# Two chained 3x3 convolutions and an attention block: every convolution as fp32 matmuls on four 64x64 tiles

## The reference

```python
for _ in range(3):
    t = relu(conv3x3(x, w1) + b1)
    x = x + (1/3) * (conv3x3(t, w2) + b2)
x = relu(x)
q, k, v = split(qkv_w @ x)              # 8 heads of 8 channels
k, v = layernorm(k), layernorm(v)       # over the 8 channels of a head
kv = sum over pixels of k (x) v / (64*64)
ret = q @ kv + x
u = gelu(o1_w @ ret)
out = gelu(o2_w @ u + x)
```

## Time and profile before

| quantity | value |
|---|---|
| median of the runs | 1623.48 us |
| span of the profiled execution | 1619.8 us |
| PE busy | 1581.7 us (98%) |
| VectorE (DVE) busy | 1090.7 us (67%) |
| ScalarE (ACT) busy | 751.2 us (46%) |
| GpSimd busy | 85.9 us (5%) |

### The profile page before, as it was taken

One profiled execution on the slowest core, in us unless ns is written; L12 is line 12 of the kernel. 1 busy time (PEld: TensorE's weight loads), 2 busy tenths in 40 slices (PEclk: granted clock), 3 DMA queues, 4 the chain that ended last, 5 costly groups with the idle time before them and its releaser, 6 DMA issues.

```text
span 1619.8 us, 25740 instructions
## 1 busy us (share of the span) xinstructions
PE 1581.7 (98%) x9339; PEld 1372.0 (85%) x9339; DVE 1090.7 (67%) x2060; ACT 751.2 (46%) x1322; POOL 85.9 (5%) x107
## 2 busy tenths in 40 slices
PE   7999999999999999999999999999999999999975
PEld 6999988888988889888898888988898879988862
DVE  5565687556875577765767667775587665876574
ACT  4333544436443464435643446433464334543454
POOL 0000000000000000000000000000000000000000
PEclk9999999999999999999999999999999999999997
DMA  6212332333322234122421235122531233112312
GB/s 114 53 26 53 53 53 40 62 57 53 66 40 53 53 55 77 27 52 53 80 52 27 52 66 92 27 39 49 90 60 27 40 59 59 27 27 53 69 37 52
DMA packets 149190, 85.98 MB, mean 53 GB/s; under 512 B 136652, under 2 KB 136652, under 8 KB 149068
## 3 DMA queue, kind: packets, MB, share of 16 engines
q0 software_dynamic: 13824, 50.34, 17.3%
...
## 4 chain that ended last, share of the span: by engine, by line
PE 93%; DVE 3%; ACT 2%; issue 1%; DMA 1%; SPq 0%; ACTq 0%; DVEq 0%
PE bank L930 30%; PE bank L889 18%; PE bank L891 16%; PE bank L890 16%; PE bank L977 4%; PE bank L989 4%; PE bank L1023 2%; PE bank L1036 2%; DMA out<-y_out 0%; SPq L387 0%; PE bank L1007 0%; DVE rstd L791 0%; ACT g L541 0%; DVE x_lo L652 0%; ACT x_in L536 0%
## 5 line engine op out<-in xcount | busy, mean ns | idle before, releaser
L889 PE MATMUL bank<-x_hi,w_hi 128*128 128x448 f32 (+2 forms) x1440 | 526.3, 365 | 3.5 <-DVE x_lo L652 3.3
L930 PE MATMUL bank<-v_all,fw 128*128 128x256 f32 x2304 | 517.1, 382 | 1.0 <-DVE v_all L731 0.6
L891 PE MATMUL bank<-x_hi,w_lo 128*128 128x448 f32 (+2 forms) x1440 | 509.3, 354 | 0.0
L890 PE MATMUL bank<-x_lo,w_hi 128*128 128x448 f32 (+2 forms) x1440 | 508.6, 353 | 0.0
L930 PEld LDWEIGHTS bank<-v_all,fw 128*128 128x128 f32 x2304 | 431.7, 190 | 73.7 <-ACT m L506 9.7
L889 PEld LDWEIGHTS bank<-x_hi,w_hi 128*128 128x128 f32 x1440 | 272.0, 189 | 48.3 <-issue 22.8
L891 PEld LDWEIGHTS bank<-x_hi,w_lo 128*128 128x128 f32 x1440 | 271.5, 189 | 15.2
L890 PEld LDWEIGHTS bank<-x_lo,w_hi 128*128 128x128 f32 x1440 | 271.6, 189 | 13.6
L493 ACT ACTIVATE t_eo<-bank,b_col 128x384 f32<-128x384 f32 (+2 forms) x240 | 141.6, 590 | 301.5 <-PE bank L891 300.9
L716 DVE TENSOR_TENSOR steps_q<-t_eo 128x1344 f32<-128x1344 f32 x96 | 119.9, 1249 | 193.4 <-ACT t_eo L493 193.4
L506 ACT ACTIVATE m<-bank 128x512 f32<-128x512 f32 x192 | 114.2, 602 | 167.7 <-PE bank L930 167.6
...
## 6 DMA issues: line engine op xcount, KB each, us to landing
...
out<-y_out SPq DMA_DIRECT2D x120, 128.0 KB, 2.7
...
b_col<-in_L_conv_b SPq DMA_DIRECT2D x4, 0.2 KB, 2.8
...
```

Source lines behind the costliest of these rows:

```text
L889: mm(ps, lhs[0], rhs[0], start=first, stop=False)
L890: mm(ps, lhs[0], rhs[1], start=False, stop=False)
L891: return mm(ps, lhs[1], rhs[0], start=False, stop=last)
L930: last = mm(ps, fw[:, q, 1 - stack, :], v_all[:, KEPT.index(q), g0 + stack:g0 + stack + size, :], start=stack == 0, stop=stack == 1)
```

## The change

**Layout.** The two images of a pair stand side by side in the partitions: image 0 in partitions 0 to 63, image 1 in 64 to 127, each with all its rows in the free dimension (`xs`, rows of 66 elements). The array is used as four independent 64x64 tiles.

**conv0** (`convolve_conv0`, line 703 of the new kernel). Nine taps, each a 64x64 fp32 matmul on 8 rows of 64 columns; the four tiles hold two images by two "sides", rows 8b.. from the top and rows from the bottom upwards. A block is 9 x 4 matmuls of 512 columns, in two parts of five and four taps; an image pair has four blocks. There are no high and low parts any more.

**conv1** (`convolve_conv1`, line 727). The transform now runs down the rows: four rows from six planes, three column taps each. A unit is two planes, that is 2 x 3 x 4 matmuls of 256 columns; three units are one half of the pair of images, and two halves are the whole. The upper side's data stand in partitions 0 to 63 and the lower side's in 64 to 127. VectorE transforms a half in seven instructions (lines 521 to 541) and combines a half in nine (lines 550 to 583), for both images together.

**Order.** No loop is left; everything is written out. `phases` names, for each round `it`, six phases over three pairs in flight: conv0 of the new pair's step 0, conv1 of the old pair's step 1, conv1 of the new pair's step 0, conv0 of the old pair's step 2, conv0 of the new pair's step 1, conv1 of the old pair's step 2. They have 8, 6, 6, 8, 8 and 6 gaps, 42 in all (0 to 41). Attention of pair it-2 follows the gaps by `LATE` (round 8, in which no new pair starts, by `LAST`; round 9 has attention alone). `TRANSFORMS` says at which gap VectorE transforms which half. The convolutions have two PSUM buffers of two banks, and PROJECT, UP and DOWN share one buffer of two banks (`ring_free`).

```diff
-CONV0_SIZES = (7, 7, 7, 6, 6)
...
+X_RING, V_RING = 3, 3
+PLANES = (1, 2, 3, 4, 0, 5)
...
+def phases(it):
+    new, old = it, it - 1
+    both = [(CONV0, new, 0), (CONV1, old, 1), (CONV1, new, 0), (CONV0, old, 2), (CONV0, new, 1), (CONV1, old, 2)]
+    return [p if 0 <= p[1] < PAIRS else None for p in both]
...
+TRANSFORMS = {5: (0, 0), 10: (0, 1), 25: (3, 0), 27: (3, 1), 33: (4, 0), 38: (4, 1)}
...
+LATE = {
+    1: steps(PIXELS, 0), 2: steps(PROJECT, 0) + steps(PIXELS, 1), 3: steps(PROJECT, 1), 4: steps(PROJECT, 2) + steps(PIXELS, 2),
+    5: steps(PROJECT, 3), 6: steps(PIXELS, 3), 7: steps(DEVIATION, 0), 8: steps(INVERT, 0), 9: steps(NORMALISE, 0, 1),
+    10: steps(NORMALISE, 2, 3) + steps(OUTER, 0), 11: steps(OUTER, 1, 2), 12: steps(OUTER, 3) + steps(PROJECT, 4),
+    14: steps(PROJECT, 5), 15: steps(RELU, 0), 16: steps(PROJECT, 6), 17: steps(RELU, 1), 18: steps(PROJECT, 7),
+    19: steps(DEVIATION, 1),
+    20: steps(INVERT, 1), 21: steps(NORMALISE, 4, 5), 22: steps(NORMALISE, 6, 7) + steps(OUTER, 4),
+    23: steps(OUTER, 5, 6), 24: steps(OUTER, 7), 25: steps(FOLD, 0), 26: steps(FOLD, 1), 27: steps(FOLD, 2),
+    28: steps(FOLD, 3) + steps(UP, 0), 29: steps(DOWN, 0) + steps(FINISH, 0),
+    30: steps(UP, 1), 31: steps(DOWN, 1) + steps(FINISH, 1), 32: steps(UP, 2), 33: steps(DOWN, 2) + steps(FINISH, 2),
+    34: steps(UP, 3), 35: steps(DOWN, 3) + steps(FINISH, 3),
+}
...
+            def drain_conv1(unit):
...
+                if part < 2:
+                    if part == 0 and half:
+                        act.wait_ge(sums_made, half)
...
+            def transform_t(unit, h, combined):
...
+                dve.wait_ge(drained, NUMBER[unit] + 1)
...
+                vec.tensor_tensor(q[:, :, :], rows[:, at + 2:at + 18, :], rows[:, at:at + 16, :], ALU.subtract
+                                  ).then_inc(t_read, 1)
...
+                vec.scalar_tensor_tensor(eo[:, :, :, :], centre, -4.0, ahead, ALU.mult, ALU.add).then_inc(t_read, 1)
...
+                vec.scalar_tensor_tensor(to[:, :, 2], step[:, :, 1], 2.0, step[:, :, 2], ALU.mult, ALU.add)
+                vec.scalar_tensor_tensor(to[:, :, 3], step[:, :, 1], -2.0, step[:, :, 2], ALU.mult, ALU.add)
+                vec.scalar_tensor_tensor(to[:, :, 4:6], step[:, :, 0:2], -4.0, step[:, :, 2:4], ALU.mult, ALU.add)
...
+                vec.tensor_tensor(to[:, :, 0], eo[:, :, 1, :], eo[:, :, 0, :], ALU.add)
+                vec.tensor_tensor(to[:, :, 1], eo[:, :, 1, :], eo[:, :, 0, :], ALU.subtract).then_inc(v_made, 1)
...
+            def combine_m(unit, h, transformed):
...
+                dve.wait_ge(drained, NUMBER[unit])
+                vec.tensor_tensor(sums[:, 0:2, :], m[:, 0:4:2, :], m[:, 1:4:2, :], ALU.add)
+                vec.tensor_tensor(sums[:, 2:4, :], m[:, 0:4:2, :], m[:, 1:4:2, :], ALU.subtract
+                                  ).then_inc(sums_made, 1)
...
+            for it, gap, unit, sub in GAPS:
+                if gap in TRANSFORMS and phases(it)[TRANSFORMS[gap][0]]:
+                    nth, h = TRANSFORMS[gap]
+                    transform_t((*phases(it)[nth], BLOCKS - HALVES + h), h, combined)
+                    transformed += 1
+                if unit and sub == 1:
+                    if unit[0] == CONV1 and unit[3] % PARTS == PARTS - 1:
+                        combine_m(unit, unit[3] // PARTS, transformed)
+                        combined += 1
...
+                for s in todo(it, gap):
+                    attention(it - 2, s)
...
-            def three(ps, lhs, rhs, first, last):
-                mm(ps, lhs[0], rhs[0], start=first, stop=False)
-                mm(ps, lhs[0], rhs[1], start=False, stop=False)
-                return mm(ps, lhs[1], rhs[0], start=False, stop=last)
+            def bank_free(unit):
+                if NUMBER[unit] >= 2:
+                    pe.wait_ge(drained, NUMBER[unit] - 1)
+            def convolve_conv0(unit, sub):
...
+                for tap in (range(0, 5), range(5, K * K))[sub]:
+                    r, c = tap // K, tap % K
+                    top = slice(8 * b + r, 8 * b + r + 8)
+                    last_row = ROWS - 1 - 8 * b + r
+                    bottom = slice(last_row, last_row - 8, -1)
+                    for side, rows in enumerate((top, bottom)):
+                        for p in range(2):
+                            half = slice(CH * p, CH * p + CH)
+                            last = mm(to[CH * side:CH * side + CH, BANK * p:BANK * p + BANK], w1_t[half, tap, :],
+                                      tile[half, rows, c:c + COLS], start=tap == 0, stop=tap == K * K - 1)
+                if sub == 1:
+                    last.then_inc(conv_ready, 1)
+            def convolve_conv1(unit):
+                _conv, a, s, k = unit
+                h, part = k // PARTS, k % PARTS
+                half = HALVES * FIRST[a, s] + h
+                if part == 0:
+                    if half == 0:
+                        pe.wait_ge(weights_made, 1)
+                    pe.wait_ge(v_made, half + 1)
+                bank_free(unit)
+                to = conv_ps[NUMBER[unit] % 2]
+                for j in range(2):
+                    place = 2 * part + j
+                    product = PLANES[place]
+                    for c in range(K):
+                        for i in range(2):
+                            for side in range(2):
+                                rows = slice(CH * side, CH * side + CH)
+                                tiles = slice(0, TILES) if side == 0 else slice(TILES - 1, None, -1)
+                                at = BANK * side + SPAN * j
+                                last = mm(to[CH * i:CH * i + CH, at:at + SPAN], fw[rows, product, c, :],
+                                          v[half % V_RING][rows, tiles, place, i, c:c + COLS],
+                                          start=c == 0, stop=c == K - 1)
+            def ring_free(a, s):
...
+                b, kind, k = RING[r - 1]
+                if kind == PROJECT:
+                    pe.wait_ge(proj_taken, 8 * b + k + 1)
+                elif kind == UP:
+                    pe.wait_ge(gelu_done, 4 * b + k + 1)
+                else:
+                    pe.wait_ge(down_added, 4 * b + k + 1)
```

More of the change, by code:

```diff
@@ L70 @@
[L70 to L106, removed]
@@ L109 @@
[L109 to L124, removed]
@@ L126 @@
[L126 to L146, removed]
@@ new lines @@
+UNITS = [unit for _it, _gap, unit, sub in GAPS if unit and sub == 1]
+NUMBER = {unit: n for n, unit in enumerate(UNITS)}
+CONV0S = [u[:3] for u in UNITS if u[0] == CONV0 and u[3] == 0]
+CONV1S = [u[:3] for u in UNITS if u[0] == CONV1 and u[3] == 0]
+assert [u[1:] for u in CONV0S] == [u[1:] for u in CONV1S]
+FIRST = {u[1:]: n for n, u in enumerate(CONV0S)}
+TRANSFORMS = {5: (0, 0), 10: (0, 1), 25: (3, 0), 27: (3, 1), 33: (4, 0), 38: (4, 1)}
+PIXELS, PROJECT, DEVIATION, INVERT, NORMALISE, OUTER, FOLD, UP, DOWN, FINISH, RELU = (
+    "pixels", "project", "deviation", "invert", "normalise", "outer", "fold", "up", "down", "finish", "relu")
@@ new lines, in steps @@
+def steps(kind, *numbers):
+    return [(kind, k) for k in numbers]
+LATE = {
[10 more added lines that the diff above has]
+}
@@ L185, in conv_attention_kernel, with todo @@
+def todo(it, gap):
+    table = LAST if it == PAIRS else LATE
+    return table.get(gap, []) if 0 <= it - 2 < PAIRS else []
+RING = [(it - 2, *s) for it, gap, _unit, _sub in GAPS for s in todo(it, gap) if s[0] in (PROJECT, UP, DOWN)]
+PROJECTED = (0, 1, 6, 7, 2, 3, 4, 5)
 def conv_attention_kernel(nc, x, w1, b1, w2, b2, qkv_w, o1_w, o2_w, kln_w, kln_b, vln_w, vln_b, out):
-    x_v = x.rearrange("(i k) c (j p) w -> i k p c j w", k=2, p=2)
-    out_v = out.rearrange("(i k) c (j p) w -> i k p c j w", k=2, p=2)
@@ L852, in _ @@
-            iteration(0, attends=False, splits=True, first=True)
-            with dve.Fori(1, PAIRS - 1) as i:
-                iteration(i, attends=True, splits=True)
-            iteration(PAIRS - 1, attends=True, splits=False)
-            attention(PAIRS - 1, LAST, RING_LAST)
+                for side, (near, far) in enumerate(((0, 2), (2, 0))):
+                    half = slice(CH * side, CH * side + CH)
+                    vec.tensor_copy(to[5][half], rows[far][half])
+                    last = vec.tensor_copy(g_first[half], rows[near][half])
@@ new lines, in _ @@
+            transpose_w1()
+            pe.wait_ge(w1_copied, 1)
+            for it, gap, unit, sub in GAPS:
+                if unit and unit[0] == CONV0:
+                    convolve_conv0(unit, sub)
+                elif unit:
+                    convolve_conv1(unit)
+                if (it, gap) == (0, 1):
+                    transpose_w2()
+                if (it, gap) == (0, 3):
+                    transpose_rest()
+                for s in todo(it, gap):
+                    attention(it - 2, s)
```

1147 lines of the change are left out of this document (455 added, 692 removed).

## The result

The changed kernel takes **1717.39 us** (median of four runs, 1716.16 to 1720.5) against 1623.64 us (1620.92 to 1625.59) of the kernel before in the same comparison. The ratio is 1.0582, with a 95% interval of 1.0565 to 1.0599: 5.8% slower, 3.4 us above the forecast of 1714. The profiled execution has a span of 1714.7 us, at a mean granted clock of 0.915.

A forecast was written before the change was run, and what follows sets the result against it. TensorE alone bounds the kernel. Rounds sum 99 + 154 + 1230 (six of 205: 165 work, 32 waits, 8 clock) + 130 + 97 = 1710 us span, with 3.7 around it 1714 us; eight-in-ten range 1590 to 1830.

The forecast's parts named there:

- (a): Gaps 10 and 11: TensorE waits before OUTER 0 and OUTER 2 for VectorE's NORMALISE chain, 12.3 us a round.
- (b): Gap 26: FOLD 1 waits for VectorE's copy after FOLD 0, behind the transform of gap 25, 4.1 us.
- (c): Gap 28: FOLD 3 waits behind the transform of gap 27, then UP 0 for the `gw` copy, 5.3 us.
- (d): Gap 34: UP 3 waits for VectorE's addition for DOWN 2, behind the transform of gap 33, 4.7 us.
- (e): Gap 41: ScalarE may not overwrite `m` until sums behind the transform of gap 38 are made, 5.8 us.
- clock: TensorE runs at half clock after each of five waits in a full round, costing 8 us.
- Round 1: Round without attention: 139.7 us of convolution plus waits at gaps 13 and 41 and clock, 154 us.
- Round 0: First round, no old pair: start near 7, 1.7 for cold clock, convolutions, exposed combination and transfer, ending at 99 us.
- Round 8: Round with no new pair: 62 us of convolution, 25.6 of attention, waits and some cold clock, 130 us.
- Rival 2: Convolutions: rows of 66 elements or four streams slow matmuls by 11%, 123 us on top, about 1800 us; chance 0.2.
- Rival 3: Convolutions: weight loads, 0.13 us in each four-tile round, come into the open, 450 us, total 2100; chance 0.06 (or worse).
- Rival 1: Middle rounds: no waits to speak of, 165 to 175 us each, 1478 us total; chance 0.22 with partial cases.

The follow-up runs named there:

- x7_both28: x3_last with VectorE's transform of gap 27 moved to gap 28, behind that gap's attention steps: 1514.31 us, ratio 0.9322 to the kernel before.
- x1_norm: Changed kernel with NORMALISE 2 and 3 moved from gap 10 to gap 9, ahead of the transform and combination: 1667.87 us.
- x5_gap10: Changed kernel with four unneeded VectorE reductions added ahead of the transform of gap 10 in rounds 2 to 7: 1739.09 us.
- x2_fold: Changed kernel with the transforms of gaps 25, 27 and 33 placed behind their gap's attention steps: 1633.97 us.
- x8_fold28: x2_fold with the transform of gap 27 moved to gap 28, behind that gap's attention steps: 1589.51 us.
- x3_last: Changed kernel with the transform behind combination and attention in every gap, and NORMALISE 0 to 3 at gap 9: 1549.0 us.
- x9_warm42: Changed kernel with 42 idle matmuls ahead of the wait before OUTER 2 in rounds 2 to 7: 1709.11 us.

## Why the prediction was right

**Bound and work.** The forecast rested on TensorE's work falling to 165 us a full round; PE is busy 168.74 in x7_both28's round, at full clock. The convolutions are exact where they stand alone (0.43 and 0.22 us a round of four). So is the attention: in x7_both28's round its steps, from start to start and without waits, sum to 25.8 us, where 25.6 stood. The 3.5 us missing lie in the convolution's groups next to a step of another tile shape. Eight rounds of conv0 take 3.43 us from start to start between UP and DOWN, and 3.61 between two PROJECTs:

```profile
541.79 3.63 PE L703 MATMUL ps<-xs,w_t 64*64 64x512 f32 x32
545.22 1.05 PE L802 MATMUL ps<-g,o 64*64 64x512 f32 x8
...
603.57 3.68 PE L703 MATMUL ps<-xs,w_t 64*64 64x512 f32 x32
607.18 1.16 PE L757 MATMUL ps<-kvw,y 64*128 64x128 f32 x16
```

The prediction had seen this cost (0.16 us at a change of shape) and then left it out of its sum for PROJECT, OUTER and FOLD.

**The waits**, term by term, per middle round:

| step | priced | measured | tested by |
|---|---|---|---|
| (a) OUTER 0 and 2 at gaps 10, 11 | 12.3 | 1.2 + 10.6 | x1_norm, x5_gap10 (the 10.6) |
| (b) FOLD 1 | 4.1 | 3.8 | x2_fold |
| (c) FOLD 3 and UP 0 | 5.3 | 4.6 + 0.3 | x2_fold, x8_fold28 |
| (d) UP 3 | 4.7 | 4.4 | x2_fold |
| (e) gap 41, `sums_made` | 5.8 | 2.15 | gone in x3_last and x7_both28, never moved alone |
| clock | 8 | 9.0 (PE busy 177.75, less 168.74 in x7_both28) | x9_warm42, for one place |

The waits sum to 27, not 32. **The mis-sized term is (e).** I let the whole transform of gap 38 wait for `conv_ready`. VectorE's timeline of the changed kernel says otherwise, and ScalarE's drain comes earlier for it:

```profile
639.59 2.35 DVE L521 TENSOR_TENSOR q<-t 128x2112 f32<-128x2112 f32 x1
641.85 1.25 DVE L528 SCALAR_TENSOR_TENSOR eo<-t 128x1056 f32<-128x1056 f32 x1
646.27 0.71 DVE L536 SCALAR_TENSOR_TENSOR v<-q 128x528 f32<-128x528 f32 x1 [3.17 <-PE ps L727]
...
651.06 1.22 DVE L551 TENSOR_TENSOR sums<-m 128x1024 f32<-128x1024 f32 x1
```

```profile
652.37 0.69 ACT L392 ACTIVATE m<-ps,b_third 128x512 f32<-128x512 f32 x1 [5.07 <-DVE sums L551]
```

Only the third instruction, L536, writes `v` and waits (3.17 us, for TensorE); the first two, 3.5 us, need only the drain of conv0 and ran ahead. That accounts for 3.5 of the 3.65 us between priced and measured.

The other errors cancel: 165 + 32 + 8 = 205 was too low by 3.7 in the work and about 1 in the clock, and too high by 5 in the waits. Round 1, with the (e) kind of wait alone, came out 8 us shorter for the same reason: its two waits are 2.17 and 2.15 us, together 7.3 less than priced. Round 0 was 5 us longer: the first conv0 waited until 11.3 us and not 7, for `in_x`. The 1.7 us priced there for the cold clock have no row behind them, and the profile does not show them as such: it grants 1.00 from 11.2 to 21 us, although TensorE did 28 instructions of conv0 in the first 5.8 us and 44 in the 4.0 us behind them. Why it was slow there stays open. Round 8 was 9 us longer, and not by its waits: PE is idle for 37 us of it, where 39 stood, but busy 101.9 us, where 87.6 and 3.4 for the clock stood, at a granted clock of 0.84. A forecast 3.4 us off is partly luck; what the experiments bear out is the mechanism and each of its places.

**Rival 2** (rows of 66 elements slow the matmul by 11%) is refuted: rounds of 0.43 us are those of the contiguous groups of the earlier trace rows. So rows of 66 elements as such do not slow an fp32 matmul. Whether the slower starts of the old form come from its format or from its rows in that format, no run tells apart.

**Rival 3** (loads in the open) is refuted: each round of conv1 brings four loads, 135 ns each by the page's L727 row below, and the rounds start 0.22 us apart:

```profile
L727 PEld LDWEIGHTS ps<-v,fw 64*64 64x64 f32 x6912 | 280.9, 135 | 132.0 <-ACT m L393 22.2
```

The Trainium skill (TensorE: Matmul & The Clock Gate, Part 3) says in its list of what overlaps that a load overlaps running matmuls only when their row groups differ. By that rule 0.13 us should show in every round; this trace does not agree, and the measurement decides. The same part of the Trainium skill, under its mechanism, also lets a load be pulled ahead when it goes into the background weight buffer; that sentence fits the trace.

**Rival 1** (no waits to speak of) priced a full round at 165 to 175 us. That is x7_both28's 171.7: the work allowed it, the order did not. The point named as deciding it, where NORMALISE 2 stands, holds the longest single wait, and moving it alone gave 50 us of the 203 between the changed kernel and x7_both28.

What the walk missed altogether is the copy to `gw` behind the transform of gap 27: priced at 0.6 us and shown at 0.3, but 4.4 us a round lay behind it, covered by the wait for FOLD 3. It did not touch the forecast and cost two expectations.
